# A cross-attention and FFN kernel on one core: the third stage's pipeline made one step shorter

## What is computed

```python
x = x + _L0_xattn_ref(_layernorm(x), ctx, ctx, W_diff, ..., W1, b1, W2, b2)
x = x + _L0_ffn_ref(_layernorm(x), weight, bias)
# _L0_xattn_ref, after the attention has given f_diff:
h = _layernorm(f_diff, ln_g, ln_b)
mlp = jax.nn.gelu(h @ W1.T + b1, approximate=False) @ W2.T + b2   # 128 -> 512 -> 128
out = mlp + f_diff
return _layernorm(out, ln_g, ln_b)
# _L0_ffn_ref:
x_mat = quantize_e4m3(x2d, SCALE).astype(jnp.float16)              # fp8
w_mat = quantize_e4m3(weight, SCALE).astype(jnp.float16)
out2d = (x_mat @ w_mat.T).astype(jnp.float32) + bias
```

## Time and profile before

| | |
|---|---|
| median of 3 runs | 262.85 us (261.82 to 263.94) |
| the profiled execution | 263.03 us, of which its span (first to last instruction) 261.2 us |
| PE busy (matmuls) | 210.6 us, 81% of the span |
| DVE busy | 223.6 us, 86% |
| ACT busy | 203.3 us, 78% |
| POOL busy | 163.9 us, 63% |
| mean granted TensorE clock | 0.938 |

### The profile page before, as it was taken

The page is one execution under the profiler, slowest core; times in us unless marked ns, Lnnn a source line. Parts: engine busy times, 40 slices in busy tenths (PEclk is TensorE's granted clock), DMA queues, the critical chain, the costliest instruction groups (busy, mean ns, idle before and its releaser), DMA issues.

```text
span 261.2 us, 5843 instructions
## 1 busy us (share of the span) xinstructions
PE 210.6 (81%) x1723; PEld 177.2 (68%) x1723; DVE 223.6 (86%) x873; ACT 203.3 (78%) x740; POOL 163.9 (63%) x208
## 2 busy tenths in 40 slices
PE   2775766854498888888899999999999999998422
PEld 1754645543386666665688999898989889987410
DVE  2899999989879999999534787999999999899994
ACT  4599999998579999997876577877877777777522
POOL 2577766766676555446813559966677776667572
PEclk9999998895579999999999999999999999999955
DMA  5676544430000000002172144999888898888695
GB/s 143 195 216 189 166 147 147 146 99 1 1 0 3 3 0 5 0 3 31 12 80 30 15 49 57 134 145 138 126 124 109 118 129 127 128 120 122 103 168 135
DMA packets 51888, 23.92 MB, mean 92 GB/s; under 512 B 9872, under 2 KB 51728, under 8 KB 51856
## 3 DMA queue, kind: packets, MB, share of 16 engines
q0 software_dynamic: 16384, 8.13, 28.7%
q1 hardware_dynamic: 35040, 15.21, 21.9%
q10 hardware_dynamic: 432, 0.20, 0.3%
HBM read 9.37 MB, written 4.19 MB: 52 GB/s over the span
## 4 chain that ended last, share of the span: by engine, by line
PE 48%; ACT 33%; issue 7%; DMA 5%; DVE 3%; POOL 3%; SPq 0%; ACTq 0%; POOLq 0%; DVEq 0%
PE bank L926 22%; ACT TQK L497 6%; ACT TQK L470 6%; ACT TQK L454 6%; PE bank L917 6%; PE bank L918 5%; PE bank L919 5%; PE bank L907 3%; ACT PV L465 3%; DMA LN_c<-in_ctx_dram 2%; ACT vT_c L459 2%; ACT vT_c L534 2%; DMA F<-rows 2%; ACT E_c L516 2%; ACT LN_c L506 2%
## 5 line engine op out<-in xcount | busy, mean ns | idle before, releaser
L926 PE MATMUL bank<-W2T,TQK 128*128 128x128 f32 x512 | 68.3, 279 | 0.8 <-ACT TQK L492 0.4
L926 PEld LDWEIGHTS bank<-W2T,TQK 128*128 128x128 f32 x512 | 64.4, 191 | 5.8 <-ACT TQK L492 1.3
L492 ACT ACTIVATE TQK<-bank,b1c 128x512 f32<-128x512 f32 (+1 forms) x68 | 44.4, 660 | 19.3 <-PE bank L919 18.5
L366 POOL TENSOR_SCALAR q_c<-TQK,GAINK,SHIFT 128x128 f32<-128x128 f32 x64 | 32.5, 519 | 23.7 <-PE bank L970 23.1
L917 PE MATMUL bank<-hTh,W1h 128*128 128x512 f32 (+1 forms) x68 | 30.3, 445 | 0.2 <-issue 0.2
L348 POOL TENSOR_TENSOR xrstd<-xvar,pow_c 128x4 f32<-128x4 f32 x16 | 16.8, 1051 | 21.2 <-DVE xvar L645 21.2
L375 POOL DMA_DIRECT2D F<-rows x17 | 25.7, 1511 | 4.5 <-DVE E_c L715 4.4
L919 PE MATMUL bank<-hTh,W1l 128*128 128x512 f32 (+1 forms) x68 | 26.0, 382 | 0.0
L918 PE MATMUL bank<-hTl,W1h 128*128 128x512 f32 (+1 forms) x68 | 26.0, 382 | 0.0
L413 POOL TENSOR_TENSOR ovar<-sso,eps_c 128x4 f32<-128x4 f32 (+1 forms) x17 | 5.1, 297 | 33.2 <-ACT TQK L568 33.2
L875 PE MATMUL bank<-WdT,vT_c 128*128 128x128 f32 x128 | 21.3, 317 | 5.7 <-ACT vT_c L459 5.4
(11 more groups left out here) (124 smaller groups left out, 608.9 us busy)
## 6 DMA issues: line engine op xcount, KB each, us to landing
F<-rows POOLq DMA_DIRECT2D x30, 256.0 KB, 4.9
LN_c<-in_ctx_dram SPq DMA_DIRECT2D x16, 256.0 KB, 2.9
X<-in_x_dram SPq DMA_DIRECT2D x16, 256.0 KB, 3.2
out_dram<-F SPq DMA_DIRECT2D x15, 256.0 KB, 4.1
LN_c<-in_L_xattn_W_dram SPq DMA_DIRECT2D x1, 256.0 KB, 3.8
lT_c<-in_L_xattn_W_dram SPq DMA_DIRECT2D x1, 256.0 KB, 4.0
F<-rows POOLq DMA_DIRECT2D x2, 128.0 KB, 4.6
out_dram<-F SPq DMA_DIRECT2D x2, 128.0 KB, 2.3
```

Source lines behind the costliest of these rows:

```text
L366: last = pool.tensor_scalar(tile(diff_c, k, i), all_tile(TK, k, i), per_tile(GAINK, k, i), per_tile(SHIFT, k, i), ALU.mult, ALU.add)
L492: act.activation(hid(m, j), m1_bank(m, j), ACT.Gelu, bias=b1c[:, j:j + 1]).then_inc(gelu_ready, 1)
L926: last = pe.matmul(M2_B[m.buf][:, i * D:(i + 1) * D], hid(m, j)[:, i * D:(i + 1) * D], W2T[:, j * D:(j + 1) * D], start=(j == 0 and i == 0 ...
```

## The change

DVE quantises a piece in the step of its residual (lag 3), at the very end of the step, with the six small statistics all ahead of it in one go; `result` comes right before it. POOL's power leads its step (lag 3), ahead of that of the output, and everything that hangs on `xq_ready` goes to lag 3 too, the two wide operations with it. The cast and the transposing DMA go to lag 3, the FFN product to lag 4, `result` and the store to lag 5, and for the last three pieces to lag 4 (`last_of`). On ACT the copy L587 (now `rounded`) moves for pieces 0 to 13 from the end of a step to a place between `upper_half` and the squares of the next. No instruction on data is added or removed.

```diff
--- before.py
+++ after.py
@@ -185,6 +185,9 @@
         D_B, L_B, S_B, EP_B = bank[2], bank[3], (bank[4], bank[7]), (bank[5], bank[6], bank[1])
         M1_B, M2_B, HT_B, XQ_B, FF_B = (bank[2], bank[3], bank[7]), (bank[4], bank[1]), bank[0], bank[5], bank[6]
 
+        def last_of(at):
+            return [k for k in (at(5), at(4)) if k.live and (k.n >= XQ_HERE) == (k is at(4))]
+
         def chunk(t, k):
             return t[:, k.at * D:(k.at + k.g) * D]
 
@@ -312,17 +315,16 @@
             sp.dma_start(Wf_raw, Wf).then_inc(wf_in, 16)
 
             def phase3(at):
-                k = at(4)
+                for k in last_of(at):
+                    sp.wait_ge(y_ready, k.n + 1)
+                    sp.dma_start(out_d[:, k.at:k.at + k.g], tiles(chunk(F, k))).then_inc(stored, 16)
+                k = at(3)
                 if k.live and k.n < XQ_HERE:
                     sp.wait_ge(xq16_ready, k.n + 1)
                     wait(sp, ff_ps, k.n - 1)
                     sp.dma_start_transpose(tiles(buf(xqT_c, k)), buf(xq16_c, k)).then_inc(xqT_in[k.buf], 16)
-                k = at(6)
-                if k.live:
-                    sp.wait_ge(y_ready, k.n + 1)
-                    sp.dma_start(out_d[:, k.at:k.at + k.g], tiles(chunk(F, k))).then_inc(stored, 16)
-
-            run_steps(pieces, 6, phase3)
+
+            run_steps(pieces, 4, phase3)
             sp.wait_ge(stored, 16 * NP)
 
 
@@ -406,6 +408,12 @@
                 k = at(0)
                 if k.live and k.n > 0:
                     add_b2(k)
+                x1 = at(3)
+                if x1.live:
+                    pool.wait_ge(x1_var, x1.n + 1)
+                    wait(pool, xq_ready, x1.n - 1)
+                    pool.tensor_tensor(buf(xrstd, x1, G), buf(xvar, x1, G), pow_c[:, 0:x1.g],
+                                       ALU.pow).then_inc(x1_rstd, 1)
                 k = at(2)
                 if k.live:
                     pool.wait_ge(ovar_ready, k.n + 1)
@@ -414,27 +422,22 @@
                     pool.wait_ge(oeps_ready, k.n + 1)
                     pool.tensor_tensor(buf(orstd, k, G), buf(ovar, k, G), pow_c[:, 0:k.g],
                                        ALU.pow).then_inc(orstd_ready, 1)
-                k = at(4)
-                if k.live and k.n < BF_HERE:
-                    pool.wait_ge(xq_ready, k.n + 1)
-                    pool.dma_start(tiles(chunk(F, k)), over_tiles(bf_r, k.g), accum_op=ALU.add).then_inc(bf_added[k.n % 3], 16)
-                if is_piece(k, 0):
+                if x1.live:
+                    pool.wait_ge(xq_ready, x1.n + 1)
+                    if x1.n < BF_HERE:
+                        pool.dma_start(tiles(chunk(F, x1)), over_tiles(bf_r, x1.g),
+                                       accum_op=ALU.add).then_inc(bf_added[x1.n % 3], 16)
+                    else:
+                        pool.tensor_tensor(tiles(chunk(F, x1)), tiles(chunk(F, x1)), over_tiles(bf_r, x1.g),
+                                           ALU.add).then_inc(bf_done, 1)
+                if is_piece(x1, 0):
                     late = slice(EARLY * G, T)
                     pool.wait_ge(fvar_ready, NA)
                     pool.tensor_tensor(VARF[:, late], VARF[:, late], eps_c[:, :], ALU.add).then_inc(feps_ready, 1)
                     pool.wait_ge(feps_ready, 1)
                     pool.tensor_tensor(RSTDF[:, late], VARF[:, late], pow_c[:, :], ALU.pow).then_inc(frstd, 1)
-                k3 = at(3)
-                if k3.live:
-                    pool.wait_ge(x1_var, k3.n + 1)
-                    wait(pool, xq_ready, k3.n - 1)
-                    pool.tensor_tensor(buf(xrstd, k3, G), buf(xvar, k3, G), pow_c[:, 0:k3.g], ALU.pow).then_inc(x1_rstd, 1)
-                if k.live and k.n >= BF_HERE:
-                    pool.wait_ge(xq_ready, k.n + 1)
-                    pool.tensor_tensor(tiles(chunk(F, k)), tiles(chunk(F, k)), over_tiles(bf_r, k.g),
-                                       ALU.add).then_inc(bf_done, 1)
-
-            run_steps(pieces, 4, phase3)
+
+            run_steps(pieces, 3, phase3)
 
 
         @block.scalar
@@ -550,8 +553,13 @@
             run_steps(pairs, 2, phase2)
 
 
+            def rounded(q):
+                act.wait_ge(ff_ps, q.n + 1)
+                wait(act, y_ready, q.n - 1)
+                act.activation(buf(r16_c, q), FF_B[:, 0:q.g * D], ACT.Copy).then_inc(r16_ready, 1)
+
             def phase3(at):
-                h, m, o, c, q = at(0), at(1), at(2), at(4), at(5)
+                h, m, o, c = at(0), at(1), at(2), at(3)
 
                 if m.live and m.n > 0:
                     gelu(m, 0)
@@ -561,6 +569,9 @@
                     act.activation(WfT[:, :], XQ_B[:, 0:D], ACT.Copy).then_inc(wf_sb, 1)
                 if h.live and h.n > 1:
                     upper_half(h)
+                q = at(5)
+                if q.live and q.n < XQ_HERE:
+                    rounded(q)
                 if o.live:
                     act.wait_ge(o_ready, o.n + 1)
                     wait(act, oeps_ready, o.n - 1)
@@ -577,16 +588,14 @@
                     if c.n > 1:
                         act.wait_ge(xqT_in[c.buf], 16 * (c.n // 2))
                     act.activation(buf(xq16_c, c), buf(xq_c, c), ACT.Copy).then_inc(xq16_ready, 1)
+                q = at(4)
                 if q.live and q.n >= XQ_HERE:
                     act.wait_ge(xqT_ps, q.n - XQ_HERE + 1)
                     wait(act, ff_ps, q.n - 1)
                     act.activation(buf(xqT_c, q), XQ_B[:, 0:q.g * D], ACT.Copy).then_inc(xqT_sb, 1)
-                if q.live:
-                    act.wait_ge(ff_ps, q.n + 1)
-                    wait(act, y_ready, q.n - 1)
-                    act.activation(buf(r16_c, q), FF_B[:, 0:q.g * D], ACT.Copy).then_inc(r16_ready, 1)
-
-            run_steps(pieces, 5, phase3)
+                    rounded(q)
+
+            run_steps(pieces, 4, phase3)
 
 
         @block.vector
@@ -810,44 +819,30 @@
                 dve.tensor_tensor(chunk(F, y), buf(r16_c, y), chunk(F, y), ALU.add).then_inc(y_ready, 1)
 
             def phase3(at):
-                h, o, x1, q, y = at(0), at(2), at(3), at(4), at(6)
+                h, o, x1 = at(0), at(2), at(3)
                 if h.live:
                     if is_piece(h, EARLY):
                         dve.wait_ge(frstd, 2)
                     if h.n > 1:
                         take_h(h)
-                    if o.live:
-                        output(o)
-                    if x1.live:
-                        residual(x1)
-                        x1_moments(x1)
-                    if q.live:
-                        quantise(q)
-                    if x1.live:
-                        wait(dve, x1_rstd, x1.n - 1)
-                        stats_terms(x1, x1_bn, x1_halves)
-                    if h.n > 1:
-                        lower_half(h)
-                    if x1.live:
-                        stats_halves(x1, x1_halves, x1_terms)
-                        stats_var(x1, x1_terms, x1_var)
-                else:
-                    if o.live:
-                        output(o)
-                    if x1.live:
-                        residual(x1)
-                        x1_moments(x1)
-                        wait(dve, x1_rstd, x1.n - 1)
-                        stats_terms(x1, x1_bn, x1_halves)
-                        stats_halves(x1, x1_halves, x1_terms)
-                        stats_var(x1, x1_terms, x1_var)
-                    if q.live:
-                        quantise(q)
-                if y.live:
+                if o.live:
+                    output(o)
+                if x1.live:
+                    residual(x1)
+                    x1_moments(x1)
+                    wait(dve, x1_rstd, x1.n - 1)
+                    stats_terms(x1, x1_bn, x1_halves)
+                    stats_halves(x1, x1_halves, x1_terms)
+                    stats_var(x1, x1_terms, x1_var)
+                if h.live and h.n > 1:
+                    lower_half(h)
+                for y in last_of(at):
                     result(y)
+                if x1.live:
+                    quantise(x1)
 
             dve.wait_ge(xb_ready, NC)
-            run_steps(pieces, 6, phase3)
+            run_steps(pieces, 4, phase3)
 
 
         @block.tensor
@@ -980,7 +975,7 @@
             run_steps(pairs, 2, phase2)
 
             def phase3(at):
-                h, m, q = at(0), at(1), at(5)
+                h, m, q = at(0), at(1), at(4)
                 if m.live and m.n > 0:
                     mlp1(m, 0)
                     mlp1(m, 1)
```

## The result

| | before | after |
|---|---|---|
| median | 263.39 us (261.82 to 264.51) | 267.71 us (267.08 to 268.49) |
| the profiled execution | 263.03 us, span 261.2 | 267.08 us, span 265.3 |

A forecast was written before the change was run, and what follows sets the result against it. PE was taken to set the full steps (7.25 us), so gains could come only from the end; 263.03 + 1.9 (step 4) + 2.6 (last steps) = 267.5 profiled, 267.4 us median, 1.7% slower, 8-in-10 range 265.0 to 270.8.

The forecast's parts named there:

- The full steps: Steady steps: DVE's step 7.10 us, under PE's 7.25, and ACT's moved copy hidden by a few hundredths; loss 0.
- One of the signs named: In the trace of after, ACT's moved copy would bring no longer wait of PE's loads of L926.
- Step 4: First term: POOL's wide operations delay pow(1), q(1) and piece 5's `take_h`, so PE's transposes wait; 1.9 us, bounds 1.5 to 2.5.
- The idle in front of q(1): Sign on DVE: q(1) (L808) with an idle of about 2.5 us put down to POOL.
- The last steps: Second term: y(14) waits for its bias DMA with piece 16's chain queued behind; last y 2.6 us later, bounds 1.6 to 3.4.
- Not slower: Rival at the end: piece 14's bias DMA lands before DVE reaches y(14); tail term 0.3, time 265.2 us; chance 0.12.
- Faster: Rival at the end: the shorter pipeline frees 3 us; 261.9 us, or 260 with wide operations hidden; chance 0.08.
- The full step stretches: Rival: eleven full steps each 0.1 to 0.45 us longer, by engine exclusion or lacking cover; around 270.5 us; chance 0.18.
- the rule: GpSimd and DVE contend when DVE has two SBUF inputs, so x1's power would end after `result`; sum about 271 to 272.

The follow-up runs named there:

- Run 9: run 1 plus, in full steps, a second ACT copy of 384 product columns to a spare tile ahead of each product copy: 270.64 us, ratio 1.0281 to before.
- run 1: Changed kernel with POOL's two 24-column operations moved from behind piece 0's bias DMA to behind add_b2 of piece 3: 265.92 us, ratio 1.0100 to before.
- run 4: Changed kernel with the wide operations behind add_b2 of piece 3, and y(14) and y(15) behind q(16): 264.53 us, ratio 1.0066 to before.
- run 5: run 1 with last steps fused: output(16) ahead of q(14), residuals 15 and 16 together, then q(15), y(14), q(16), y(15), y(16); POOL reordered: 263.89 us, ratio 1.0041.
- run 6: run 5 with y(12) and y(13) moved behind the statistics of piece 15: 263.79 us, ratio 1.0028 to the kernel before.
- run 11: run 1 with `result` ahead of `lower_half`, so that y runs beside POOL's power in each full step: 269.13 us by two executions, ratio 1.0213 to before.
- run 7: Changed kernel with the bias of piece 14 added by a POOL operation instead of the DMA: 268.42 us, ratio 1.0164 to the kernel before.
- run 8: Kernel before with the bias of piece 14 added by a POOL operation instead of the DMA: 263.61 us, ratio 1.0007.

## Why the prediction was right

**The full steps** came as counted: 7.10 us from `output` to `output` where DVE is behind (158.27 to 165.37), under PE's 7.24, and no loss from the copy on ACT. One of the signs named did not come: PE's loads of gelu 2's output do wait now, 0.29 us in each full step, where they had no wait before. It costs nothing, since the 16 loads behind it take 1.88 us, and took 2.14 before. Run 9 shows that the cover was a matter of hundredths.

**Step 4**, predicted 1.9, is 2.09 in the trace and 2.0 by run 1. The chain is the one told. Q(1) starts 15.17 behind the `output` of step 3 (156.63 - 141.46), predicted 14.91 (157.25 - 142.34), and PE's loads were 1.82 late. The catching up inside DVE's spare was right too: PE has no gap in the later full steps. The delay alone is 1.87, though; the other 0.22 is the earlier FFN product of run 1, which the prediction left out. The idle in front of q(1) is 3.41 and not about 2.5, for the 2.5 left out the 0.55 us that q(1) waits for its power anyway (run 1), and the power was 0.3 later.

**The last steps**, predicted 2.6, are 3.29, the term that was mis-sized. Counted from the `output` of step 16:

| us | predicted | measured |
|---|---|---|
| q(14) starts | 11.5 | 12.11 |
| bf(14) issued | 12.8 | 13.88 |
| y(14) starts | 18.2 | 18.30 |
| residual of piece 16 | 19.35 | 19.42 |
| its variance done | 21.8 | 22.35 |
| q(16) starts | 22.7 | 23.40 |
| last y ends | 25.55 | 26.20 |

Two misses cancel ahead of y(14). Pow(14) took 1.41 us and not 1.0, beside y(12), and POOL issued bf(14) 0.65 us after q(14) had ended (248.92 + 1.12 = 250.04 to 250.69), where I took a tenth; but the DMA landed in 4.42 us (250.69 to 255.11), near the low end of its bounds, and not in the 5.44 of the earlier trace rows. A tenth is left at y(14), and 0.55 is added behind it: 0.46 in the residual of piece 16, which took 1.07 instead of 0.61, and about 0.15 in front of q(16). Before the store, the terms so sum to 5.4 instead of 4.5; the spans differ by only 4.10 since after began the stage 0.88 earlier and its store ended 0.40 faster. The medians are 4.3 apart. The hit of the total to 0.3 us is thus in part luck: the two terms were 0.9 too small together.

**The rivals.** *Not slower* asked for a landing in 3.1 us; it took 4.42. *Faster* fell with the order of DVE and POOL, as told, and runs 4 to 6 add why it doesn't come true in a better order either: with y(14) late and the wide operations early the shorter pipeline is still 0.7% slower, and each of the last quantises waits for its own power. Filling these waits (runs 5 and 6) gave back 1.3 of the 1.9 us. *The full step stretches* did not happen, but its mechanism is real. In the full steps of after the power took 1.03 us although `result` started inside it, and in step 16 ended inside it too, as below: the forecast there was right. Where y starts just ahead of the power, it took 1.41: pow(14) at 247.41, since no `lower_half` is left to stand between the variance and y, and every full step of run 11. I judged the last steps by the durations of the full ones, and that is where 0.4 and 0.46 us were missed.

DVE, then POOL of after, in step 16 a y and the power beside it:

```profile
241.32 0.68 DVE L819 TENSOR_TENSOR F<-LN_c,F 128x512 f32<-128x512 f16 x1
```

```profile
241.16 1.03 POOL L415 TENSOR_TENSOR xrstd<-xvar,pow_c 128x4 f32<-128x4 f32 x1 [2.09 <-DVE xvar L654]
```

The trace of before had a row of this kind, which the prediction did not look at when it said that the trace leans against the rule. Orstd of piece 15 began 0.1 us behind an add of DVE with two SBUF inputs and took 1.15 us, where that of piece 16 took 0.70. DVE, then POOL of before:

```profile
242.92 0.69 DVE L784 TENSOR_TENSOR F<-X,F 128x512 f32<-128x512 f32 x1
```

```profile
243.02 1.15 POOL L415 TENSOR_TENSOR orstd<-ovar,pow_c 128x2 f32<-128x2 f32 x1
...
249.47 0.70 POOL L415 TENSOR_TENSOR orstd<-ovar,pow_c 128x2 f32<-128x2 f32 x1
```

The Trainium skill (GPSIMD Engine Reference, section 1, Specifications) has GpSimd and VectorE contend over SBUF when a DVE instruction has "two SBUF inputs". The traces agree for this orstd, pow(14), the residual of piece 16 and runs 7, 8 and 11, and differ for the power at 241.16, which a y inside its time didn't lengthen.
